# Tokens on ScalarE, and all expert scalings of the second mixture on GpSimd

## The reference, cut to what matters

```python
xt = x.reshape(-1, embed_dim)            # x comes in normalised: (x - mean) / sqrt(var + 1e-5)
logits = xt @ w_gate
top_logits, sel = jax.lax.top_k(logits, TOP_K)
probs = jax.nn.softmax(top_logits, axis=-1)
h = silu(einsum('td,edh->eth', xt, w1)) * einsum('td,edh->eth', xt, w3)
y = einsum('eth,ehd->etd', h, w2)
out = einsum('ktd,tk->td', y[sel.T, t], probs)
```

## Time and profile before

| what | us |
|---|---|
| time, median of 3 runs (lowest, highest) | 2728.72 (2727.49, 2733.39) |
| the profiled execution, its own time | 2731.78 |
| span of the profiled execution | 2730.0 |
| busy: TensorE, VectorE, GpSimd, ScalarE | 2443.1, 1947.8, 1487.3, 1378.8 |
| moe0 layers, about | 450 to 640, 960 to 1160 |
| moe1 layers, about | 1553 to 1872, 2406 to 2730 |
| mean granted TensorE clock | 0.934 |

### The profile page before, as it was taken

One profiled execution on the slowest core, in us unless ns is written; L12 is line 12 of the kernel. 1 busy time (PEld: TensorE's weight loads), 2 busy tenths in 40 slices (PEclk: granted clock), 3 DMA queues, 4 the chain that ended last, 5 costly groups with the idle time before them and its releaser, 6 DMA issues. The chain is left out here.

```text
span 2730.0 us, 39978 instructions
## 1 busy us (share of the span) xinstructions
PE 2443.1 (89%) x12716; PEld 1542.4 (56%) x12716; DVE 1947.8 (71%) x4454; ACT 1378.8 (51%) x2168; POOL 1487.3 (54%) x1371
## 2 busy tenths in 40 slices
PE   4477997998789989989999889998999999979998
PEld 3344565666656556644444467775444444347776
DVE  6865775775667667756666598886777778668887
ACT  4632453333435523256666445553777677645554
POOL 5924654443265534366666456655667566336654
PEclk8688898998869999989999999998999999789999
DMA  1001111221021032110000211110000000021221
GB/s 48 0 3 30 35 36 56 94 94 50 1 49 40 14 111 94 70 57 1 1 1 1 69 46 56 63 55 24 1 1 1 2 1 1 1 89 56 70 67 43
DMA packets 57512, 104.49 MB, mean 38 GB/s; under 512 B 15192, under 2 KB 30424, under 8 KB 57048
## 3 DMA queue, kind: packets, MB, share of 16 engines
q1 hardware_dynamic: 57304, 101.90, 11.7%
HBM read 86.53 MB, written 2.62 MB: 33 GB/s over the span
## 5 line engine op out<-in xcount | busy, mean ns | idle before, releaser
L2327 DVE TENSOR_REDUCE l_diffneg_max<-psum 128x1 fp32r<-128x512 f32 x512 | 336.0, 685 | 98.2 <-PE psum L2065 89.5
L4464 POOL TENSOR_TENSOR l_moe1sc<-l_moe1s,l_moe1bcs 128x512 f32<-128x512 f32 x192 | 276.5, 1453 | 218.1 <-ACT l_moe1s L4280 198.7
L2242 ACT ACTIVATE l_diffweights<-psum 128x1024 f32<-128x1024 f32 x256 | 261.7, 1025 | 142.3 <-PE psum L2094 141.4
L4280 ACT ACTIVATE l_moe1s<-psum 128x512 f32<-128x512 f32 x256 | 152.9, 598 | 231.5 <-PE psum L851 230.3
L2065 PE MATMUL psum<-l_diffkz,l_diffQ 128*128 128x512 f32 (+1 forms) x512 | 239.2, 486 | 2.9 <-DVE l_diffneg_max L2327 2.0
L4366 DVE TENSOR_TENSOR x<-l_moe1sc,psum 128x512 f32<-128x512 f32 x256 | 174.5, 682 | 89.2 <-POOL l_moe1sc L4464 60.0
L4373 DVE TENSOR_TENSOR l_moe1g_lo<-x,l_moe1g_hi 128x512 fp32r<-128x512 f32 x256 | 230.1, 900 | 0.1
L2866 ACT ACTIVATE l_lightswapped<-psum 32x512 f32<-32x512 f32 x304 | 178.7, 588 | 101.8 <-DVE l_lightturned L2958 98.3
L1592 DVE TENSOR_REDUCE l_attn0neg_max<-psum 128x1 fp32r<-128x512 f32 x256 | 167.3, 683 | 52.7 <-PE psum L1326 50.0
L173 POOL TENSOR_TENSOR settled<-powers 128x1 f32<-128x1 f32 x111 | 31.4, 283 | 302.4 <-DVE l_alibimv L698 72.0
L4280 ACT ACTIVATE l_moe0s<-psum 128x512 f32<-128x512 f32 x144 | 86.1, 598 | 211.7 <-PE psum L851 187.8
(11 more groups left out here) (583 smaller groups left out, 6749.5 us busy)
## 6 DMA issues: line engine op xcount, KB each, us to landing
l_moe0bcs<-gate_rows SPq DMA_DIRECT2D x64, 512.0 KB, 4.6
l_moe1bcs<-gate_rows SPq DMA_DIRECT2D x64, 512.0 KB, 3.8
l_attn0Q<-l_attn0q_hi SPq DMA_DIRECT2D x128, 64.0 KB, 2.0
l_moe1w_raw<-in_moe_w SPq DMA_DIRECT2D x20, 256.0 KB, 6.7
l_attn0Q<-l_attn0q_lo SPq DMA_DIRECT2D x64, 64.0 KB, 2.0
l_moe0w_raw<-in_moe_w SPq DMA_DIRECT2D x20, 128.0 KB, 5.1
x<-in_x SPq DMA_DIRECT2D x8, 256.0 KB, 4.5
out<-x SPq DMA_DIRECT2D x8, 256.0 KB, 2.3
```

The costliest lines, as they stand in the source:

```text
L2242: nc.scalar.activation(weights[:, tt, 2 * pair:2 * pair + 2, :], ps[:, S[m % 2]:S[m % 2] + 2, :], ACT.Exp, scale=SCALE).then_inc(act_exp.s ...
L2327: nc.vector.tensor_reduce(neg_max[:, n % 2, st, row:row + 1], ps[:, bank_of(("max", n, b)), :], AXX, ALU.max, negate=True).then_inc(vec_ma ...
L4280: nc.scalar.activation(s[:, n % 2, h, :], ps[:, H1[(n * HT + h) % 2], :], ACT.Silu).then_inc(act_silu.sem, act_silu.step("silu", h))
L4464: nc.gpsimd.tensor_tensor(sc[:, n % 2, h, :], s[:, n % 2, h, :], weights_row(n), ALU.mult).then_inc(pool_sc.sem, pool_sc.step("sc", h))
```

## The change

ScalarE makes z in both kinds. In moe1 it is one activation for each 128 tokens with scale and bias (Identity, scale = 1/sqrt(var + eps), bias = -mean times that), four a sequence; GpSimd makes this bias (`shift`), with one more small product and `-mean`. In moe0 it is four copies with a scale. They stand behind slot 3 of ScalarE's program in moe1 and behind slot 7 in moe0; for sequence 1 they stand at the start of the layer, ahead of ScalarE's rounding of the weights. `token_scale` stays on GpSimd, behind slot 1 (in sequence 0 of moe1: behind slot 2 instead of 3). `on_pool` now holds for all slots of moe1, so that GpSimd does all 16 scalings of a sequence.

```diff
-    on_pool = lambda n: not moe.shared and n % NE not in (1, 3)
+    on_pool = lambda n: not moe.shared
...
-    AT_STATS, AT_SCALE, AT_Z = (3, 6, 7) if moe.shared else (4, 1, 1)
-    FIRST_Z = 7 if moe.shared else 3
+    AT_STATS, AT_SCALE, AT_Z = (3, 6, 7) if moe.shared else (4, 1, 3)
...
         @block.scalar
         def _(a):
...
+            def tokens(j):
+                act_z.start()
+                a.wait_ge(pool_scale.sem, pool_scale.done(j, "scale" if kind == "rms" else "shift"))
+                a.wait_ge(pe_tr.sem, pe_tr.done(j, "tr", back=1))
+                for q in range(NQ):
+                    of = src[:, j * T + q * P:j * T + (q + 1) * P]
+                    if kind == "rms":
+                        ins = nc.scalar.activation(z[:, q, :], of, ACT.Copy, scale=scale[:, q:q + 1])
+                    else:
+                        ins = nc.scalar.activation(z[:, q, :], of, ACT.Identity, bias=shift[:, q:q + 1], scale=scale[:, q:q + 1])
+                ins.then_inc(act_z.sem, act_z.step("z"))
...
+            tokens(1)
             weights_in.scalar_group(a, 0)
...
+                if e == AT_Z and j + 2 < NSEQ:
+                    tokens(j + 2)
...
         @block.gpsimd
         def _(p):
...
                 else:
+                    inc(nc.gpsimd.tensor_scalar(square[:, :], mean, -1.0, None, ALU.mult), "minus_mean")
                     inc(nc.gpsimd.tensor_scalar(var2[:, :], var, LN_EPS, None, ALU.add), "var2")
                 wait("var2")
                 inc(nc.gpsimd.tensor_tensor(scale[:, :], var2[:, :], core.half, ALU.pow), "scale")
...
-                if kind == "rms":
+                if kind == "ln":
                     wait("scale")
-                    inc(nc.gpsimd.tensor_tensor(z[:, :, :], tokens_of(src, j), spread(scale[:, :]), ALU.mult), "z")
-                else:
-                    inc(nc.gpsimd.tensor_tensor(z[:, :, :], tokens_of(src, j), spread(mv[:, j % 2, :, 0]), ALU.subtract), "centred")
-                    wait("centred")
-                    inc(nc.gpsimd.tensor_tensor(z[:, :, :], z[:, :, :], spread(scale[:, :]), ALU.mult), "z")
+                    inc(nc.gpsimd.tensor_tensor(shift[:, :], square[:, :], scale[:, :], ALU.mult), "shift")
...
-                if j + 2 < NSEQ:
-                    if e == (AT_SCALE if j else min(FIRST_Z, 6)):
-                        token_scale(j + 2)
-                    if e == (AT_Z if j else FIRST_Z):
-                        tokens(j + 2)
-                if opening and j == NSEQ - 2 and e == FIRST_Z:
+                if j + 2 < NSEQ and e == (AT_SCALE if j else AT_Z - 1):
+                    token_scale(j + 2)
+                if opening and j == NSEQ - 2 and e == AT_Z:
                     opening.scale(p)
                     opening.tokens(p)
```

More of the change, by code:

```diff
@@ L4067, in moe_block @@
         pe_down, act_out, pe_tail, vec_tail = steps("_down_tensor"), steps("_out_scalar"), steps("_tail_tensor"), steps("_tail_vector")
-        vec_stats, pool_z = steps("_statistics_vector"), steps("_tokens_pool")
+        vec_stats, pool_scale, act_z = steps("_statistics_vector"), steps("_scale_pool"), steps("_tokens_scalar")
         pe_tr, act_hi, vec_lo = steps("_head_tensor"), steps("_head_scalar"), steps("_head_vector")
@@ L4074, in moe_block @@
         square, var2, scale = sb("square", [P, NQ]), sb("var2", [P, NQ]), sb("scale", [P, NQ])
-        mean_square = sb("mean_square", [P, NQ])
+        mean_square, shift = sb("mean_square", [P, NQ]), sb("shift", [P, NQ])
         free = src is core.x
@@ L4091, in moe_block @@
         opening = core.opening
-        for of in (vec_stats, pool_z, pe_tr, act_hi, vec_lo):
+        for of in (vec_stats, pool_scale, act_z, pe_tr, act_hi, vec_lo):
             of.skip_first()
@@ L4230, in head_turned @@
                 misc_free(t, ("tr", j))
-                t.wait_ge(pool_z.sem, pool_z.done(j, "z"))
+                t.wait_ge(act_z.sem, act_z.done(j, "z"))
                 for q in range(NQ):
@@ L4264, in _ @@
         def _(a):
-            for of in (act_silu, act_ghi, act_out, act_hi, chooser.act_comb):
+            for of in (act_silu, act_ghi, act_out, act_hi, act_z, chooser.act_comb):
                 of.credit(a)
             copy = lambda to, frm: nc.scalar.activation(to, frm, ACT.Copy)
+            def tokens(j):
[9 more added lines that the diff above has]
+                ins.then_inc(act_z.sem, act_z.step("z"))
             def head_hi(j):
@@ L4333, in statistics @@
                 if j >= 2:
-                    d.wait_ge(pool_z.sem, pool_z.done(j - 2, "z"))
+                    d.wait_ge(pool_scale.sem, pool_scale.done(j - 2, "scale" if kind == "rms" else "shift"))
                 d.wait_ge(vec_stats.sem, vec_stats.done(j, "stats", NQ - 1))
@@ L4421, in _ @@
         def _(p):
-            for of in (pool_sc, pool_z, chooser.pool_ex, chooser.pool_e2, pool_added):
+            for of in (pool_sc, pool_scale, chooser.pool_ex, chooser.pool_e2, pool_added):
                 of.credit(p)
-            spread = lambda m: m.unsqueeze(2).to_broadcast([P, NQ, P])
             def token_scale(j):
-                pool_z.start()
-                inc = lambda ins, *key: ins.then_inc(pool_z.sem, pool_z.step(*key))
-                wait = lambda *key: p.wait_ge(pool_z.sem, pool_z.done(j, *key))
+                pool_scale.start()
+                inc = lambda ins, *key: ins.then_inc(pool_scale.sem, pool_scale.step(*key))
+                wait = lambda *key: p.wait_ge(pool_scale.sem, pool_scale.done(j, *key))
                 mean, var = mv[:, j % 2, :, 0], mv[:, j % 2, :, 1]
                 p.wait_ge(vec_stats.sem, vec_stats.done(j, "mean", NQ - 1))
-                p.wait_ge(pool_z.sem, pool_z.done(j, "z", back=1))
+                p.wait_ge(act_z.sem, act_z.done(j, "z", back=1))
                 settle(core, p)
@@ L4443, in token_scale @@
                 inc(nc.gpsimd.tensor_tensor(scale[:, :], var2[:, :], core.half, ALU.pow), "scale")
[L4445 to L4448, removed]
-                if kind == "rms":
-                    wait("scale")
-                    inc(nc.gpsimd.tensor_tensor(z[:, :, :], tokens_of(src, j), spread(scale[:, :]), ALU.mult), "z")
-                else:
-                    inc(nc.gpsimd.tensor_tensor(z[:, :, :], tokens_of(src, j), spread(mv[:, j % 2, :, 0]), ALU.subtract), "centred")
-                    wait("centred")
-                    inc(nc.gpsimd.tensor_tensor(z[:, :, :], z[:, :, :], spread(scale[:, :]), ALU.mult), "z")
+                if kind == "ln":
+                    wait("scale")
+                    inc(nc.gpsimd.tensor_tensor(shift[:, :], square[:, :], scale[:, :], ALU.mult), "shift")
             def scale_slot(n, h):
@@ L4472, in _ @@
             token_scale(1)
-            tokens(1)
             chooser.clear(p)
```

## The result

| | before | changed |
|---|---|---|
| median of 6 runs each, us | 2731.88 | 2744.81 |
| lowest to highest, us | 2727.49 to 2734.24 | 2731.53 to 2750.18 |
| ratio | 1 | 1.0047, interval 1.0029 to 1.0065 |
| profiled execution: time, span, clock | 2731.78, 2730.0, 0.934 | 2731.53, 2729.7, 0.940 |

The account below looks back on a forecast made before the run. TensorE, 89% busy, was taken to lose time in moe1 where VectorE bounds the stretch of choosing experts. Terms 11.9 + 2.0 + 1.0 = +14.9 us on the 2728.7 median gave 2743.6 us, range 2727 to 2757.

Parts of the forecast that it names:

- slot 3 behind the power: In moe1, slot 3's scaling queues on GpSimd behind a power waiting for VectorE: +1.08 us a period, +11.9 for 11.
- slot 1's chain on GpSimd: In moe1, GpSimd's work at slot 1 ends just when slot 2's scaling used to start: 0 to 0.3 us, taken as 0.
- race of slot 3's low half: VectorE's low half of slot 3 against GpSimd's scaling of slot 5: GpSimd wins as before, so no difference.
- first sequences: First sequence of either moe1 layer, slot 3's scaling behind statistics and token work: bounds 0 and +3.3 us, +2.0 for two.
- sequence 6 of layer 7: Slot 4's scaling 0.5 us later, slot 3's low halves 1.0 later, with TensorE at its lower clock there: +1.0 us.
- tokens on ScalarE, moe0: ScalarE's token copies ahead of slot 8's silu in moe0: up to +4 us, less 1 for VectorE, taken as 0.
- the waits that the view shows for TensorE: Sign in a moe1 period: TensorE's stalls sit in the same two slots and sum to 1.1 us more.
- later stalls stay and shift, GpSimd wins: Behind slot 2's second low half in moe1, every offset stays the old one: the two later stalls shift by 1.08 us.
- no change: Rival: VectorE wins the race behind slot 3, a period costs 0, sum +2 to +3, 2731 us; chance 0.17.
- Near the lower end since the later stall takes most of it up: In each moe1 layer's first sequence, the stall at slot 4 absorbs most of slot 3's delay: +1.0 us taken.
- tokens that are not hidden: Rival: the tokens' activations on ScalarE are not hidden: +4 to +8 us, 2748 to 2752; chance 0.07.
- Clock: Rival: longer stalls drop TensorE to its lower clock in each choice stretch: +17.6 us more, 2761; chance 0.08.

Follow-up runs that it names:

- again: The changed kernel run once more with no edit: median 17.8 us over before's, ratio 1.0049.
- slot1_on_vector: Against the changed kernel, the scalings of slot 1 go back to VectorE: median 11.1 us over before's, ratio 1.0044.
- tokens_on_scalar: Against the changed kernel, the scalings of slots 1 and 3 go back to VectorE, tokens stay on ScalarE: ratio to before 0.9999.
- slot3_on_vector: Against the changed kernel, the scalings of slot 3 go back to VectorE: median 0.2 us under before's, ratio 1.0009.
- before_scaling5_late: The kernel before, plus a GpSimd memset of 128x128 ahead of slot 5's scaling from sequence 1 on: median 7.4 us under before's, ratio 0.9983.
- low_half_late: Against the changed kernel, a VectorE memset of 128x256 ahead of slot 3's first low half: median 20.1 us over before's, ratio 1.0081.
- power_behind_slot3: Against the changed kernel, GpSimd's power stands behind slot 3's scalings, not ahead of them: median 6.0 us under before's, ratio 0.9957.

## Why the prediction was right

The mechanism of the largest term was right, and so was the total. But that the total fits within 1.4 us is luck: against the forecast, slot 1 cost 3.3 us more and the first sequences 4.5 more, while the race gave back 7.7 that the forecast left at nothing. With every race lost, as the forecast assumed, the same kernel would have been at 2754 (estimate below).

| step | forecast | measured |
|---|---|---|
| slot 3 behind the power, 11 periods | +11.9 | +11.6 (1.05 each) |
| slot 1's chain on GpSimd | 0 | +3.3 (0.30 each) |
| race of slot 3's low half, between the two kernels | 0 | -7.7 |
| first sequences | +2.0 | +6.5 (again: +7.3) |
| sequence 6 of layer 7, and the last periods | +1.0 | -0.2 |
| tokens on ScalarE, moe0 | 0 | 0 |
| sum | +14.9 | +13.5 (cut directly: +13.2) |

- **Slot 3.** Right in its links and in size, shown by 6.61 to 7.69 us, by slot1_on_vector and by moving the power. One sign did not come out as written: the waits that the view shows for TensorE were to sum to 1.1 us more. They were 1.61 in before's period from 1657.19 and are 2.33 in the lost period and 1.47 in the won one; one of these, 0.28 and 0.27, belongs to no down projection and stands behind VectorE's first product of slot 3.
- **Slot 1.** The step "ends at 1690.95, just when the scaling of slot 2 used to start, I take 0" was a term sized too small; its own bound of 0.3 was the truth. With the two scalings of slot 1 ahead of it, GpSimd's chain ends late, so that the scaling of slot 2 starts 0.6 us behind its silu, which ended at 1655.28. Half of that is the power, 1.34 us and not 1.03. It took 1.34 in each of the ten cases of this trace in which a low half of VectorE was running when it started, and 1.04 in the four in which none was. In tokens_on_scalar it takes 1.34 as well and costs nothing, so the scalings ahead of it are needed for the loss:

```profile
1654.32 1.34 POOL L4457 TENSOR_TENSOR l_moe1scale<-l_moe1var,powers 128x4 f32<-128x4 f32 x1
1655.74 0.20 POOL L4460 TENSOR_TENSOR l_moe1shift<-l_moe1square,l_moe1scale 128x4 f32<-128x4 f32 x1
1655.90 2.55 POOL L4469 TENSOR_TENSOR l_moe1sc<-l_moe1s,l_moe1bcs 128x512 f32<-128x512 f32 x2
```

  VectorE comes later by that, and TensorE pays at its stall in slot 2's down projection: 0.49 us in a won period of slot3_on_vector, nothing over 0.2 in one of tokens_on_scalar.

- **The race.** The step "later stalls stay and shift, GpSimd wins" failed: a margin of 0.03 us can't be carried over from one kernel to another. The rival "no change" had the right price, 1.1, and its 0.17 was too low for what some hundredths of a us decide in every period. It came true in 8 of 11. Before had lost 10 of 11, so 7 x 1.1 = 7.7 us came back. Had the changed kernel lost all, it would be at 2744.8 + 8 x 1.1, 2754, an estimate.
- **First sequences.** "Near the lower end since the later stall takes most of it up" holds for TensorE's idle time and misses the price. From the first product of slot 0 to the first add (before, then changed):

```profile
1563.97:1619.11 55.14, 49.41 (x209) 37.90 (x210) 48.89 (x104) 28.79 (x52) 31.69 (x27) 0.95 0.19 68
```

```profile
1561.40:1620.59 59.19, 53.21 (x210) 41.97 (x211) 43.65 (x99) 30.11 (x56) 37.23 (x33) 0.87 0.18 60
```

  TensorE idles 5.7 us before and 6.0 after, but its matmuls take 3.8 us more, since the granted clock is 0.87 in place of 0.95. In layer 9 the idle time grew by 0.5 and the busy time by 2.0, at 0.90 in place of 0.93. The forecast had the lower clock for sequence 6 and no such term here. The clock falls to its lower level behind two stalls; right behind the first of them (changed kernel):

```profile
1570.00:1577.00 7.00, 7.00 (x21) 5.70 (x21) 4.59 (x17) 2.42 (x5) 2.38 (x2) 0.52 0.14 50
```

  A place was missing in the account as well. GpSimd's scalings of slot 1 lie beside VectorE's low halves of the weights (line 4030): three took 4.04 us where before took 1.89, and TensorE waited 2.78 us for what is queued behind them, where it had 0.54. With slot 1 on VectorE it waited 1.20 and, in layer 9, under 0.5. The stall behind slot 3 grew from 1.57 to 2.92. That the clock falls because of these two stalls is read from their order; no run changed the clock alone. VectorE, TensorE, VectorE, GpSimd:

```profile
1564.77 4.04 DVE L4030 TENSOR_TENSOR l_moe1w_lo<-l_moe1w_raw,l_moe1w_hi 128x512 fp32r<-128x512 f32 x3
```

```profile
1569.56 0.25 PE L213 MATMUL psum<-open_gate,l_moe1h_hi 128*128 128x16 f32 x1 [2.78 <-DVE l_moe1h_lo L4357]
...
1587.20 0.80 PE L849 MATMUL psum<-open_hi,l_moe1w_hi 128*128 128x512 f32 x1 [2.92 <-DVE x L4380]
```

```profile
1586.46 0.69 DVE L4380 TENSOR_TENSOR x<-l_moe1sc,psum 128x512 f32<-128x512 f32 x1 [4.12 <-issue]
```

```profile
1585.11 5.87 POOL L4469 TENSOR_TENSOR l_moe1sc<-l_moe1s,l_moe1bcs 128x512 f32<-128x512 f32 x4
```

- **Sequence 6** of layer 7 took 39.27 where before took 39.75. The lower clock that the forecast counted on went away: the granted clock of this sequence was 0.96 before and is 1.00. Before with the memset took 38.12 there, at 1.00, so 1.6 us of before's 39.75 hung on the order of the two operations and on the clock. How much on each, and whether the forecast +1.0 was there beside it, was not taken apart.
- **Tokens on ScalarE.** Four activations took 1.65 us, not 1.2, ended at 1663.90, and the silu of slot 4 followed at once. Nobody waited: before_scaling5_late (tokens on GpSimd) and tokens_on_scalar have won periods of 36.95 and 37.03. So the rival of tokens that are not hidden is out, but for 0.08 us.

```profile
1662.25 1.65 ACT L4277 ACTIVATE x<-x,l_moe1shift,l_moe1scale 128x128 f32<-128x128 f32 x4
```

- **Clock.** A period with all three stalls had a granted clock of 1.00 again, so this rival fell for the periods, the only place for which it was written. In the first sequences, see above, the clock is most of what was lost:

```profile
1620.59:1660.12 39.53, 37.15 (x166) 28.70 (x165) 30.60 (x72) 21.22 (x39) 26.65 (x22) 1.00 0.16 55
```

The port rule of the Trainium skill (SBUF — State Buffer, Who interferes with whom) says that the order of issue decides who waits. The race bears it out: the low half that came second took 1.82 us in place of 0.68, and GpSimd's pair 3.55 in place of 2.98. Only in low_half_late do the recorded starts not show that order. What the Trainium skill says of offloading between VectorE and GpSimd (Perfetto Trace Analysis, Optimizing Scalar/DVE Operations), that it might not help, agrees with the 37.00 of power_behind_slot3 against the 37.03 of VectorE scaling itself.

## What to carry to other kernels

Ask of each operation moved to another engine not only whether that engine has time, but what stands ahead of it in its program: a scaling whose input was long ready stood behind a 128x4 power that waited for VectorE, and that cost more than the VectorE time it saved. Where two engines that lock each other become ready within some tenths of a us, read in several periods which of the two took longer than alone before you carry a period over, price both outcomes, and then try to decide it on purpose: 0.2 us of delay on the engine with slack gave 1.1 us a period. Where a change moves or lengthens TensorE's stalls, compare its busy time and its granted clock too, and not its idle time alone: in the first sequences idle time stayed and the clock took the time. And where one profiled execution shows no loss but the medians do, compare the stretches that the change touches.

## What the runs showed of the hardware

Starts that differ by 0.02 us or less go with either outcome of the race: a 128x512 low half took 0.68 us when it came first and 1.82 when GpSimd's scaling did. Small operations wait as well: line 296 on VectorE, 128x4, took 0.91 us beside GpSimd's pair (power_behind_slot3) and 0.15 without it, and GpSimd's 128x4 power of line 4457 took 1.34 where a low half of VectorE was running at its start and 1.04 where none was. And the same unchanged stretch of 2821 matmuls took 520.5 to 533.3 us at granted clocks from 0.97 to 0.94, as much as the whole effect of the change.
